# Strassen block products for all Q, K and V projections, stored in DRAM, ahead of attention by head and batch

## What is computed

```python
def attention(x, wq, wk, wv, wo):                    # 8 groups of 4 query heads
    q, k, v = (split_heads(x @ w.T) for w in (wq, wk, wv))
    s = where(0 <= i - j < 128, q @ k.T / sqrt(128), -inf)
    return merge_heads(softmax(s) @ v) @ wo.T
x = layernorm(x + attention(x, wq, wk, wv, wo))
x = layernorm(x + matmul(fake_quant(x), fake_quant(ctx)))
x = layernorm(x + ffn(x, w_gate, w_up, w_down))
```

## Time and profile before

| | |
|---|---|
| median of 3 runs | 1622.49 us (1621.65 to 1623.27) |
| the profiled execution | 1620.67 us, span 1618.9 us |
| PE matmul busy | 1550.2 us, 96% |
| DVE, ACT, POOL busy | 918.6, 691.5, 684.4 us |
| mean granted PE clock | 0.987 of full |
| DMA | 100.61 MB, mean 62 GB/s |

### The profile page before, as it was taken

The page is one execution under the profiler, slowest core; times in us unless marked ns, Lnnn a source line. Parts: engine busy times, 40 slices in busy tenths (PEclk is TensorE's granted clock), DMA queues, the critical chain, the costliest instruction groups (busy, mean ns, idle before and its releaser), DMA issues.

```text
span 1618.9 us, 22298 instructions
## 1 busy us (share of the span) xinstructions
PE 1550.2 (96%) x7792; PEld 1267.6 (78%) x7809; DVE 918.6 (57%) x1489; ACT 691.5 (43%) x1373; POOL 684.4 (42%) x572
## 2 busy tenths in 40 slices
PE   7999999999999999999999999986799999998897
PEld 6888888888888888888888888874567888887543
DVE  4454454355445445435544544569956676777587
ACT  4423332152242324214233331444576666667574
POOL 3425243252433515224243341545677666766100
PEclk9999999999999999999999999998999999999899
DMA  7101100110110101011011011060103233223101
GB/s 287 52 26 66 38 29 26 52 36 16 65 39 26 56 35 39 13 52 39 26 65 39 26 41 38 27 244 1 65 27 103 92 117 117 93 102 117 53 39 66
DMA packets 29438, 100.61 MB, mean 62 GB/s; under 512 B 3664, under 2 KB 4048, under 8 KB 29392
## 3 DMA queue, kind: packets, MB, share of 16 engines
q1 hardware_dynamic: 29392, 100.02, 17.9%
HBM read 94.77 MB, written 5.24 MB: 62 GB/s over the span
## 4 chain that ended last, share of the span: by engine, by line
PE 81%; DVE 10%; ACT 4%; issue 3%; POOL 1%; DMA 0%; ACTq 0%; DVEq 0%; SPq 0%; POOLq 0%
PE ps L520 10%; PE ps L522 10%; PE ps L521 10%; PE ps L598 7%; PE ps L600 7%; PE ps L599 7%; PE ps L741 6%; PE ps L742 6%; PE ps L769 5%; PE ps L539 2%; PE ps L540 2%; PE ps L538 2%; DVE u_size L1752 2%; PE ps L570 2%; PE ps L571 2%
## 5 line engine op out<-in xcount | busy, mean ns | idle before, releaser
L520 PE MATMUL ps<-xt_h,w_h 128*128 128x512 f32 x768 | 306.5, 399 | 8.3 <-DVE xt_l L1555 8.3
L1296 POOL TENSOR_TENSOR w_l<-w_raw,w_h 128x1024 fp32r<-128x1024 f32 x80 | 191.5, 2394 | 287.1 <-ACT w_h L861 287.1
L522 PE MATMUL ps<-xt_h,w_l 128*128 128x512 f32 x768 | 300.3, 391 | 0.0
L521 PE MATMUL ps<-xt_l,w_h 128*128 128x512 f32 x768 | 299.8, 390 | 0.0
L741 PE MATMUL ps<-xt_h,w_h 128*128 128x512 f32 x704 | 276.4, 393 | 7.4 <-ACT w_h L1004 7.4
L742 PE MATMUL ps<-xt_l,w_h 128*128 128x512 f32 x704 | 275.4, 391 | 0.0
L1510 DVE TENSOR_TENSOR resid<-ps,resid 128x512 f32<-128x512 f32 x256 | 176.4, 691 | 139.8 <-PE ps L600 138.5
L1304 POOL TENSOR_TENSOR pm_l<-pt_l,upto 128x512 fp32r<-128x512 f32 x64 | 82.7, 1292 | 378.9 <-DVE pt_l L1498 375.7
L598 PE MATMUL ps<-w_h,o_h 128*128 128x512 f32 x512 | 203.3, 397 | 6.8 <-DVE resid L1510 5.4
L600 PE MATMUL ps<-w_h,o_l 128*128 128x512 f32 x512 | 200.0, 391 | 0.0
L599 PE MATMUL ps<-w_l,o_h 128*128 128x512 f32 x512 | 199.8, 390 | 0.0
(11 more groups left out here) (143 smaller groups left out, 2891.3 us busy)
## 6 DMA issues: line engine op xcount, KB each, us to landing
w_raw<-w_att SPq DMA_DIRECT2D x80, 512.0 KB, 3.3
w_raw<-w_gu SPq DMA_DIRECT2D x22, 512.0 KB, 4.5
resid<-w_gu SPq DMA_DIRECT2D x22, 512.0 KB, 4.5
d_raw<-w_down SPq DMA_DIRECT2D x22, 512.0 KB, 3.2
ctx_raw<-ctx_rows SPq DMA_DIRECT2D x8, 1024.0 KB, 6.8
resid<-x_rows SPq DMA_DIRECT2D x10, 512.0 KB, 6.0
resid<-x_cols SPq DMA_DIRECT2D x16, 256.0 KB, 6.4
out<-resid SPq DMA_DIRECT2D x8, 512.0 KB, 2.6
```

The source lines that it names most:

```text
L520: pe.matmul(ps_out, wh, xt_h[:, c, rows], start=(c == 0), stop=False)
L521: pe.matmul(ps_out, wh, xt_l[:, c, rows], start=False, stop=False)
L522: last = pe.matmul(ps_out, wl, xt_h[:, c, rows], start=False, stop=(c == DC - 1))
L1296: pool.tensor_tensor(w_l[:, w, :], w_raw[:, s % 2, :], w_h[:, w, :].bitcast(F32), ALU.subtract).then_inc(w_low, 1)
```

## The change

All projections come first. Two heads' weights (256 rows, called a quad) times x are cut into 2x2 blocks in each operand: rows of head by halves of depth, halves of depth by batches. Seven block products per quad take the place of eight, in Strassen's scheme as Winograd ordered it, and there are 24 quads. Each block product is 4 chunks by 3 matmuls. DVE forms the four sums of weight blocks, ACT and POOL split the seven, and the results are put together from PSUM by ACT and DVE in c_1, c_2, c_3, c_22 and written to DRAM, four blocks of 256 KB per quad. At the start x's own four blocks are combined into seven and split: 28 chunks of 512 columns on ACT and DVE, 4 differences on DVE, 12 sums on POOL.

Attention then runs in eight slots per group, one unit per slot. A slot reloads one query block (256 KB) and splits it (ACT, POOL). The output product now sums four heads, 12 matmuls into one of four PSUM banks, two of them per slot, so that there are 128 adds in place of 256. The last two quads' 14 products run inside the first six slots. W_O is split in half-width tiles, by ACT and then POOL, after the mask in slots 4 to 7. The context is quantised in the slots 1 and 3 of groups 1 to 6 and in 1 to 4 of group 7, by ACT alone in the last step. The sizes and the output products of 6 tiles' two halves are left for the stage after attention. In the feed-forward stage new waits stand on buffers that lie elsewhere. The core of the diff:

```diff
-PROJ = 2 * BATCH + UNITS
+PRODUCTS = (PA11, PS2, PA12, PS3, PS1, PA22, PS4)
+FIRST_ORDER = (PA11, PS1, PA12, PS2, PS3, PA22, PS4)
+QUADS = (HQ + 2 * HKV) // 2
+SLOT_PRODUCTS = ((0, 1, 2), (3, 4, 5), (6, 7, 8), (9, 10), (11, 12), (13,))
...
+        prod_ps = [bank(0), bank(6), bank(0), bank(6), bank(1), bank(7), bank(1)]
+        y_ps = [bank(0), bank(1), bank(6), bank(7)]
...
+        def out_splits(j, first, last):
+            if first and j in (4, 5):
+                return [(0, h) for h in range(GROUP)] if j == 5 else []
+            if last and j in (6, 7):
+                return [(1, h) for h in range(GROUP)] if j == 6 else []
+            return [(j // 2 - 2, 2 * (j % 2) + e) for e in range(2)] if j >= 4 else []
...
         def _(pe):
-            def project(g, j, s, b):
+            def product(n, i, opening=False):
+                pe.wait_ge(w_low, block_count(n, i))
+                if i == PA12:
+                    pe.wait_ge(c1_done, n * 2 + 1)
+                if i == PS3:
+                    pe.wait_ge(sums_done, n * 5 + S_2)
+                if i == PS4:
+                    pe.wait_ge(sums_done, n * 5 + C_22)
...
+                for c in range(KH):
+                    if opening:
+                        pe.wait_ge(x_low, x_count(i, c))
...
+            def out_slot(g, j, k, last):
+                dg, b, t, half = out_block(j, k, last)
+                if k == 0 and j in (2, 6):
+                    pe.wait_ge(o_low, g * UNITS + (j - 2))
+                if k == 0 and j == 0:
+                    pe.wait_ge(wo_low, g * UNITS)
+                if k == 0 and j == 6:
...
+                    pe.wait_ge(wo_low, g * UNITS + GROUP)
+                if k == 0 and j == 7 and last:
+                    pe.wait_ge(wo_low, (g + 1) * UNITS)
+                out_product(g * 16 + (2 * j + k - 12), y_ps[(2 * j + k) % 4], t, half)
...
+            def slot_of(g, j, first, last):
+                early = first and j < 6
+                scores(g, j)
+                if early:
+                    for event in SLOT_PRODUCTS[j]:
+                        product(*late_product(event))
+                else:
+                    out_slot(g, j, 0, last)
+                if not first or j >= 2:
+                    values(g, j - 2)
+                if not first or j >= 1:
+                    turn_probs(g, j - 1)
+                if not early:
+                    out_slot(g, j, 1, last)
+                if j % GROUP == 0:
+                    turn_values(g, j // GROUP)
...
         def _(pool):
+            def slot_of(g, j, first, last):
+                if not (last and j == UNITS - 1):
+                    query_low(g, j + 1)
...
+                if not first or j >= 1:
+                    mask_probs(g, j - 1)
+                if j % GROUP == 2 and not (last and j > GROUP):
+                    key_low(g, j // GROUP + 1)
+                for half, h in out_splits(j, first, last):
+                    out_low(g, half, h)
+            block_low(0, 0, PA11)
+            block_low(0, 0, PS1)
+            for c in range(KH):
+                third_sum(c)
+                second_sum(c)
+                fourth_sum(c)
...
             def check_unit(k, i, n, checked, raw):
                 pool.wait_ge(u_made, n + 1)
+                if isinstance(checked, int) and checked == 0:
+                    pool.wait_ge(x2_low, TILES)
...
         def _(dve):
+            for c in range(KH):
+                x_rest(PA11, c)
+            block_sum(0, 0, 0, PS1)
+            for c in range(KH):
+                difference(c)
+            for c in range(KH):
+                x_rest(PS1, c)
+            block_sum(0, 0, 0, PS3)
+            block_sum(0, 0, 0, PS2)
+            for c in range(KH):
+                x_rest(PA12, c)
+            block_sum(0, 0, 0, PS4)
+            for i in (PS2, PS3):
+                for c in range(KH):
+                    x_rest(i, c)
+            second_sum(0)
+            for c in range(KH):
+                x_rest(PA22, c)
+            third_sum(0)
+            block_sum(1, 0, 1, PS3)
+            block_sum(1, 0, 1, PS2)
+            corners(0, PS1)
+            block_sum(1, 0, 1, PS1)
+            for c in range(KH):
+                x_rest(PS4, c)
...
+                softmax_bias(g, j)
+                if not events:
+                    add_slot(g, j, 0, last)
+                normalise(g, j)
...
+                    sums_low(g, j - 2)
+                    probs_low(g, j - 1)
+                if not events:
+                    add_slot(g, j, 1, last)
```

More of the change, by code:

```diff
@@ L221, in build @@
         y_added = sem("y_added")
[L222 removed]
+        ctx_loaded = [sem("ctx_loaded0"), sem("ctx_loaded1")]
         ctx_scaled = sem("ctx_scaled")
@@ new lines, in contexts, with position @@
+        def contexts(g, j, first, last):
+            if not first and not last and j in (1, 3):
+                return [(g * 2 + (j // 2 - 2), j // 2, g)]
+            if last and 1 <= j <= 4:
+                k = 2 * (HKV - 2) + j - 1
+                return [(k, k % 2, k // 2 + 1)]
+            return []
+        X11, X12, X21, X22 = range(4)
+        BLOCKS = (PA11, PA12, PS3, PS2, PS1, PA22, PS4)
+        S_2, S_3, C_22, C_21, C_12 = range(1, 6)
+        def position(n, i, first, later):
+            return (first if isinstance(n, int) and n == 0 else later).index(i) + 1
@@ new lines, in a_block, with weight_source, raw_ready @@
+        def a_block(odd, row, half):
+            return raw[odd][:, row, half * HALF:(half + 1) * HALF]
+        def weight_source(odd, i):
+            if i in (PA11, PA12, PA22):
+                return a_block(odd, int(i == PA22), int(i != PA11))
+            return s2_sum[:, :] if i == PS2 else wf_l[i][:, :]
+        def raw_ready(engine, n, r, odd):
+            if isinstance(n, int) and n == 0:
+                for part in first_raw:
+                    engine.wait_ge(part, 16)
+            else:
+                engine.wait_ge(raw_loaded[odd], r * 32 + (32 if odd else 0))
@@ L380, in _ @@
         def _(sp):
[L381 to L401, removed]
@@ L413, in _, with quad_source @@
[L413 to L427, removed]
+            def quad_source(n, row):
+                if n < HKV:
+                    return w_att[2 * n % HKV + row, n // (HKV // 2)]
+                head = 2 * (n - HKV) + row
+                return w_att[head // GROUP, 2 + head % GROUP]
@@ L431, in load_units @@
+            wait_kept(QUADS)
+            with sp.Fori(1, HKV - 1) as g:
+                for j in range(UNITS):
+                    slot(g, j, False, False)
+            for j in range(UNITS):
+                slot(HKV - 1, j, False, True)
             def load_units(c, k, i):
@@ new lines, in first_corner, with behind @@
+            def first_corner(n):
+                act.wait_ge(prod_done, product_count(n, PA12))
+                act.wait_ge(sums_done, n * 5 + S_3)
+                act.activation(c_1[:, :], prod_ps[PA12], ACT.Copy).then_inc(c1_done, 1)
+            def behind(n, i, n1, r1, odd1, make):
+                if i == PA11:
+                    first_sum(n)
+                if make and i in (PA11, PA12, PS3, PS1, PA22, PS4):
+                    block_high(n1, r1, odd1, i)
+                if i == PS3:
+                    first_corner(n)
+                    if make:
+                        block_high(n1, r1, odd1, PS2)
@@ L1466, in value_low, with behind @@
+            def behind(n, i, n1, r1, odd1, make):
+                if i == PS2:
+                    second_sum(n)
+                if i == PS3:
+                    third_sum(n)
+                    if make:
+                        block_sum(n1, r1, odd1, PS3)
+                        block_sum(n1, r1, odd1, PS2)
+                if i in (PS1, PA22, PS4):
+                    corners(n, i)
+                if make and i in (PS1, PS4):
+                    block_sum(n1, r1, odd1, i)
             def value_low(g, b):
```

1206 lines of the change are left out of this document (701 added, 505 removed).

## The result

The changed kernel takes **1680.63 us** (median of four runs, 1679.85 to 1681.43), the kernel before 1622.07 (1621.22 to 1623.27): a ratio of 1.036, 95% interval 1.0343 to 1.0378. It is slower, as forecast, but by 58.6 us instead of 25, and 4.6 us beyond the upper end of the range. The profiled execution has a span of 1679.4 us, against 1618.9 before.

What follows compares the result with a forecast made beforehand. PE was taken to bound the kernel until about 1053 us, by matmul count times distance. 1620.7 - 65.3 + 24.9 + 50.4 + 14.6 + 12.6 - 19 + 8 = 1647 us; range 1610 to 1676.

Steps and rivals of the forecast that it cites:

- Matmuls (1): Projections: 2304 matmuls become 2016, 288 fewer, for -65.3 us; output, score and value matmuls stay as many.
- steady projections (2): Quads after the opening: 19.0 us of PE work each, the other engines' work and DRAM writes hidden, costed at nothing.
- The rival of projections held by their own sums at C_22: Projection quads: 22 quads lose 1.5 us each to the C_22 sums, giving 1680; chance 0.07.
- Opening (3): Start, first quad: DVE and POOL operations hardly overlap, so PE idles 36.0 us against 11.1, +24.9.
- with idle hand-overs +33: Opening: its cost if DVE and POOL also idle at hand-overs, named beside the +24.9 used.
- Waits for W_O (4): Attention slots 0 and 6: fourteen waits of 3.6 behind POOL's mask, +50.4; longer ones in groups 0 and 7, +14.6.
- Clock (5): PE's clock after waits: long waits lose 2.8 each, two of fourteen short ones 2.1; +12.6 (8.4 to 38).
- The rival built on the same mechanism: Attention groups: the clock falls at every wait, 12 more falls at 2.1, giving 1672; chance 0.14.
- Stage after attention (6): Last slot to first feed-forward matmul: 96 us, idle 22 in place of 41, -19 (-41 to 0).
- Feed-forward start (7): POOL's first weight check stands behind x2's last low part, delaying PE's existing wait: +8 (0 to 11.6).

Runs made afterwards that it cites:

- the first edit: The changed kernel, but in the opening each engine waits only for the parts of the first quad's weights that it reads: 1672.6 us.
- both orders changed: The changed kernel with W_O's splits, outside group 0, ahead of the exponentials on ACT and ahead of the mask on POOL: 1595.32 us.
- POOL's order alone: The changed kernel with W_O's low parts ahead of the mask on POOL outside group 0, ACT's high parts left in place: 1638.67 us.
- run with fillers: The changed kernel with 44 small bf16 matmuls on PE in front of each wait for W_O's parts, nothing moved: 1652.47 us.
- the fastest kernel: The change plus the first edit, both orders changed (also group 0's slot 5), own scratch for the first four feed-forward checks, x's sums on DVE: 1575.6 us.
- the sums on DVE: The kernel with the first edit, and quad 0's twelve sums of x's blocks made by DVE in place of POOL: 1670.63 us.

## Why the prediction was off

The path in the profiled execution, against the forecast's span of 1647 - 1.8 = 1645.2: the first feed-forward matmul was expected 15.4 us later than the 1184.05 of before and came 53.0 later, at 1237.06; the rest was expected 10.8 us longer and is 7.5 longer. Together 34.3 of the 34.2 missed. The steps one by one:

- **Matmuls (1) and steady projections (2): right.** The three product lines have 672 each, and 380 us without a gap. The rival of projections held by their own sums at C_22 has no trace in it; that its time, 1680, is the one measured is chance.
- **Opening (3): mis-sized, with a cause not seen.** The first attention slot was expected at 455 and comes at 470.2, +15.2. Some 8.5 of that is the first copy's wait for weights that it does not read; the forecast had PE start as in the kernel before. It is a wait in the diff, and the step that failed was to count operations from 5.4 without asking what the first of them waits for. Without the late start, in the run with the first edit, the slot comes at 461.7 and the opening still costs 24.9 + 6.7 = 31.6. The step had named what is left ("with idle hand-overs +33") and put it at less: there DVE idles for 7.9 us behind POOL's sums. That this is the whole of the 6.7 is not shown. That DVE and POOL hardly overlap there was right: a rest and a sum side by side take 1.7 each, about 0.6 and 1.2 one behind the other. The Trainium skill ("SBUF — State Buffer", section "Who interferes with whom") says that a DVE instruction with two SBUF inputs contends with a GpSimd instruction that reads SBUF; the trace agrees, with that 1.7. Moving the sums takes 4.2 us off at quad 1.
- **Waits for W_O (4): right in place and size, the cause named by half.** 65.0 forecast, 66.5 measured; fourteen short ones at 3.6 were thirteen of 3.56 to 3.80 and one of 5.3. The step laid them to the mask ahead of the low parts on POOL. The run with both orders changed takes them away, but the one with POOL's order alone gains only half: ACT's order, which the step does not speak of, is the other half.
- **Clock (5): the step that failed most.** "I let two of fourteen fall, at 2.1." All fell, and the term in the groups, 5.6 for two long waits and 4.2 for two short ones, is 31.2 instead of 9.8: +21.4. The step rested on dense work ahead of a wait. For the 8.5 us ahead of each of the thirteen waits of 3.56 to 3.80 us PE was busy throughout at the full clock, and the clock fell behind every one. The 2.42 of the earlier trace rows was the wrong neighbour of the two. The run with fillers shows what the falls cost. The rule of the Trainium skill ("TensorE: Matmul & The Clock Gate", section "HAM oscillation"), that a gap between bursts puts the engine back each time it comes round, was borne out here in sixteen waits of sixteen, all of 3.56 us or more; behind the gaps of 0.98 and 1.28 in the run with fillers there was no fall. The rival built on the same mechanism said 1672, 25 more than the forecast where 21.4 is measured, but with the opening of the forecast.
- **Stage after attention (6): right.** 96 us from the last slot to the first feed-forward matmul were forecast; it is from 1140 to 1237, 97.
- **Feed-forward start (7): right.** The wait is 10.5, where 2.42 + 8 was forecast, and a scratch of their own for the checks takes it back to 3.4. Most of the 3.3 us by which this stage is shorter than forecast is in two places: the 16 matmuls behind the wait of 10.52 take 5.12 us, so that its fall costs 1.5 instead of 2.8, and the second wait of this line is 3.53 where it was 4.94.

So two terms carry the miss, the clock with 21.4 and the opening with 15.2. The first was written down as a rival with 0.14, on the evidence of one wait of 2.42 against two that had fallen; that evidence does not bear a weight of six to one against.

## What to carry to other kernels

Price a wait that recurs on a full TensorE at its length plus the fall of the clock behind it, here 3.6 + 1.4 to 2.5 us, unless a wait of the same length in the same trace shows otherwise. When a step makes one engine late by a few microseconds in each turn, look for the operations in front of it whose results are needed later, on that engine and on the one that feeds it, before judging the change as a whole: this one is 3.6% slower or 1.6% faster by the place of two calls. At a start read each first wait for what it covers, not only for what is read behind it.

## What the runs showed of the hardware

The clock behind short gaps of PE: there was no fall behind the thirteen waits of 0.98 and 1.28 us in the run with fillers, nor behind the 2.42 of the earlier trace rows. There was one behind 2.00 us in the fastest kernel, and one behind 2.15, at 1089.95 us in the run with POOL's order alone, where twelve output matmuls took 4.38. In the last group of the run with fillers, behind the fill, 2.85 us of idle had no fall (2.81 for the twelve) and 2.76 had one (4.36). A fall followed the 2.81 and 2.88 of the fastest kernel, six of the seven waits of 2.9 with POOL's order alone, and all thirteen of 3.56 to 3.80. So between 2 and 3 us the length alone does not decide.

Waits of the same length cost different amounts: behind 3.79 us the twelve matmuls took 4.36 us at 807.34, and behind 3.78 they took 5.12 at 725.04, so only a mean over several is a price. In the four profiled executions that have these sixteen waits (the change, the first edit, the checks' scratch, the sums on DVE) the falls behind them sum to 31.2, 29.9, 29.8 and 31.6 us.

44 small matmuls, 2.63 us, in a wait of 3.6 were enough to keep the full clock.
